# All four heads' probabilities of the second layer's attention are normalised by GpSimd, none by VectorE

## The reference

```python
def _L1_attn_ref(hidden_states, Wq, Wk_down, Wv_down, Wk_up, Wv_up, Wo):
    ...
    scores = jnp.einsum('bhqd,bhkd->bhqk', q, k) * scale
    causal = jnp.tril(jnp.ones((s, s), dtype=bool))
    scores = jnp.where(causal, scores, jnp.asarray(-1000000000.0, scores.dtype))
    attn = jax.nn.softmax(scores, axis=-1)
    out = jnp.einsum('bhqk,bhkd->bhqd', attn, v)
    out = out.transpose(0, 2, 1, 3).reshape(b, s, H * D)
    return out @ Wo.T
```

## Time and profile before

| | |
|---|---|
| median of 3 runs | 2548.25 us |
| profiled execution | 2546.12 us |
| its span, first to last instruction | 2544.3 us |
| mean granted clock of TensorE in the span | 0.956 |
| passes of the second layer's attention | 16, from about 520 to 1438 us and from about 1620 to 2544 us |

### The profile page before, as it was taken

How to read it: one execution, slowest core, us unless ns; L and a number is a source line. 1 busy time by engine, 2 the same in 40 slices (tenths; PEclk the granted TensorE clock), 3 DMA queues, 4 the chain that set the end, 5 groups by cost and what they waited for, 6 DMA issues and landing times. The chain is left out here.

```text
span 2544.3 us, 35763 instructions
## 1 busy us (share of the span) xinstructions
PE 2279.3 (90%) x11666; PEld 1818.9 (71%) x11666; DVE 1551.3 (61%) x3333; ACT 1044.3 (41%) x2182; POOL 917.7 (36%) x957
## 2 busy tenths in 40 slices
PE   5767309799999999999999797899999999999998
PEld 4623107678888888878888685687888888888886
DVE  4289995555656565665656555566565656565665
ACT  3323203344545444444445232344444545454444
POOL 2654214142525243343524101334352525343341
PEclk9879659999999999999999898999999999999999
DMA  9400003801010101010110227201011010101010
GB/s 344 137 0 1 1 35 158 325 31 38 29 49 25 58 8 58 8 58 25 41 50 1 115 92 259 83 9 58 25 41 49 16 49 25 58 8 58 8 46 29
DMA packets 71409, 159.58 MB, mean 63 GB/s; under 512 B 4416, under 2 KB 37568, under 8 KB 64832
## 3 DMA queue, kind: packets, MB, share of 16 engines
q1 hardware_dynamic: 70912, 157.44, 17.8%
q10 hardware_dynamic: 432, 1.32, 0.1%
HBM read 110.52 MB, written 69.99 MB: 71 GB/s over the span
## 5 line engine op out<-in xcount | busy, mean ns | idle before, releaser
L1439 POOL TENSOR_TENSOR probs<-probs,rinv 128x1024 f32<-128x1024 f32 (+7 forms) x384 | 439.1, 1147 | 1117.9 <-DVE rinv L1466 1117.9
L1475 DVE TENSOR_TENSOR pT<-psum,pT 128x512 fp32r<-128x512 f32 x576 | 387.1, 689 | 313.9 <-ACT pT L1515 308.6
L1509 ACT ACTIVATE probs<-psum,nmax 128x256 f32<-128x256 f32 (+7 forms) x512 | 380.7, 743 | 366.9 <-DVE nmax L1461 362.6
L1515 ACT ACTIVATE pT<-psum 128x512 fp32r<-128x512 f32 x576 | 330.3, 595 | 333.3 <-PE psum L1569 332.2
L1461 DVE TENSOR_REDUCE nmax<-psum 128x1 f32<-128x256 f32 (+7 forms) x512 | 378.1, 751 | 48.6 <-PE psum L1558 42.4
L1569 PE MATMUL psum<-ident,probs 128*128 128x128 f32 x2304 | 329.8, 273 | 8.5 <-issue 6.1
L1569 PEld LDWEIGHTS psum<-ident,probs 128*128 128x128 f32 x2304 | 263.2, 141 | 48.5 <-DVE pT L1475 9.0
L93 PE MATMUL psum<-keys,q 128*128 128x512 f32 (+3 forms) x768 | 276.7, 360 | 2.8 <-DVE q L1451 2.8
L93 PE MATMUL psum<-pT,vals 128*128 128x512 f32 x576 | 263.6, 458 | 4.0
L95 PE MATMUL psum<-keys,q 128*128 128x512 f32 (+3 forms) x768 | 262.0, 341 | 0.0
L94 PE MATMUL psum<-keys,q 128*128 128x512 f32 (+3 forms) x768 | 261.7, 341 | 0.0
(11 more groups left out here) (265 smaller groups left out, 3927.1 us busy)
## 6 DMA issues: line engine op xcount, KB each, us to landing
k_parts<-kv_out SPq DMA_DIRECT2D x32, 512.0 KB, 5.1
wq<-wq_copy SPq DMA_DIRECT2D x16, 1024.0 KB, 4.8
wo<-wo_copy SPq DMA_DIRECT2D x16, 1024.0 KB, 4.8
v_parts<-kv_out SPq DMA_DIRECT2D x32, 512.0 KB, 4.0
keys<-k_parts SPq DMA_DIRECT2D x32, 512.0 KB, 4.7
vals<-v_parts SPq DMA_DIRECT2D x64, 256.0 KB, 3.1
acc<-in_x SPq DMA_DIRECT2D x4, 1024.0 KB, 11.9
up_l<-up_copy SPq DMA_DIRECT2D x2, 1024.0 KB, 6.1
```

The costliest lines, as they stand in the source:

```text
L1439: pool.tensor_tensor(p, p, rinv[:, u, h:h + 1].to_broadcast([P, (TB - u) * P]), ALU.mult).then_inc(p_ok, 1)
L1475: dve.tensor_tensor(pT[:, n % PT_SLOTS, 1, :], bank[T_BANK + n % 2], f32(pT[:, n % PT_SLOTS, 0, :]), ALU.subtract).then_inc(t_lo, 1)
L1509: act.activation(probs[:, u % 2, h, 0:n], bank2[2 * (h % 2)][:, off:off + n], ACT.Exp, bias=nmax[:, u, h:h + 1], accum_out=rsum[:, u, h:h ...
L1515: act.activation(pT[:, n % PT_SLOTS, 0, :], bank[T_BANK + n % 2], ACT.Copy).then_inc(t_hi, 1)
```

## The change

GpSimd also multiplies head 3, in the place of the list where norm(u,3) stands. VectorE keeps the four reciprocals and loses the multiplication and its wait. TensorE waits for four counts of `p_ok` for each u in place of three of `p_ok` and one of `p_last`, and the semaphore `p_last` is gone.

```diff
@@ gpsimd
-                    if kind == "norm" and arg[1] < REP - 1:
+                    if kind == "norm":
                         u, h = arg
                         p = probs[:, u % 2, h, 0:(TB - u) * P]
                         pool.wait_ge(p_inv, it * SC + (REP * u + h + 1))
@@ vector
                         dve.reciprocal(rinv[:, u, h:h + 1], rsum[:, u, h:h + 1]).then_inc(p_inv, 1)
-                        if h == REP - 1:
-
-                            p = probs[:, u % 2, h, 0:(TB - u) * P]
-                            dve.wait_ge(p_inv, it * SC + (REP * u + h + 1))
-                            dve.tensor_scalar(p, p, rinv[:, u, h:h + 1], None, ALU.mult).then_inc(p_last, 1)
@@ tensor
                         if k == 0:
-                            pe.wait_ge(p_ok, it * ((REP - 1) * TB) + (REP - 1) * (u + 1))
-                            pe.wait_ge(p_last, it * TB + (u + 1))
+                            pe.wait_ge(p_ok, it * SC + REP * (u + 1))
```

More of the change, by code:

```diff
@@ L1217, in layer1_attention @@
         q_mm, q_hi, q_lo = sem("e_q_mm"), sem("e_q_hi"), sem("e_q_lo")
-        s_mm, s_max, p_exp, p_inv, p_ok, p_last = (sem("e_" + n) for n in ("s_mm", "s_max", "p_exp", "p_inv", "p_ok", "p_last"))
+        s_mm, s_max, p_exp, p_inv, p_ok = (sem("e_" + n) for n in ("s_mm", "s_max", "p_exp", "p_inv", "p_ok"))
         t_mm, t_hi, t_lo, pv_mm = (sem("e_" + n) for n in ("t_mm", "t_hi", "t_lo", "pv_mm"))
```

## The result

| | before | after |
|---|---|---|
| median | 2548.28 us | 2577.43 us |
| runs, lowest to highest | 2543.29 to 2548.75 | 2575.45 to 2580.6 |
| profiled execution, span | 2546.12, 2544.3 us | 2577.52, 2575.7 us |

The ratio is 1.012 with a 95% interval of 1.0103 to 1.0138: the change costs 29 us by the medians. The forecast was 2574, in a range of 2561 to 2582.

A forecast was written before the change was run, and what follows sets the result against it. TensorE was taken as the bound, busy 115.28 of 116 us a pass. Stalls of 12.2 (u = 1), 11.8 (u = 3), 0.3 (u = 0) and 2.7 us (last passes) sum to 27.0 us on 2546.12: 2574, range 2561 to 2582.

The forecast's parts named there:

- Removed: zero in the full passes: VectorE's 128 tensor_scalar instructions go; no wait of TensorE in the full passes stands behind one, so 0 us there.
- u = 1, 0.76 us x 16 = 12.2 us: wo split part 3, queued behind GpSimd's norm(1,3), ends late; project(0)'s weight load stalls 0.76 us in all 16 passes.
- u = 3, 0.84 us x 14 = 11.8 us: GpSimd's norm(3,3) queues behind wq parts 3; the transposition loads 0.84 us late in 14 passes.
- u = 0, 0.02 us x 16: GpSimd's norm queues behind norm(0,2); load possible 882.39 against 882.37, no reserve, 0.3 us in all.
- u = 2, 4, 5, 6 of a full pass, and u = 7: zero: Norms covered: 0.58 us reserve at u = 2, query products at 4 to 6, project(6)'s oT wait at 7.
- The last passes, 1.34 us each: Without query products TensorE waits for GpSimd's longer norms: 0.59, 0.45, 0.30 us at u = 4, 5, 6; 2.7 us together.
- One stall hidden: Rival: one of the two queue stalls, u = 1 or u = 3, is hidden; +15 us, 2561; chance 0.06.
- VectorE's relief: Rival: relief reaches TensorE through the pT subtraction waits, up to 24 us back; about 2540; chance 0.04.
- The whole difference of durations on the path: Rival: GpSimd's longer multiplications all delay the kernel, 128 x 0.56 us = 72 us, 2618; chance 0.01.
- GpSimd stretched in its new places: Rival: other VectorE work stretches GpSimd by 0.45 us at u = 0 and 1; 14 us more, 2588; chance 0.06.
- A balance of half the stalls and a few waits gone: Rival: half the stalls hidden and a few TensorE waits gone leave the time at 2548; chance 0.03.
- GpSimd about twice as slow: Skill's rule for two-input elementwise work against VectorE; trace said to agree, 1.04 against 0.48 us at 512 columns.

## Why the prediction was right, point by point

- **What bounds the kernel.** That a full pass has no more to give held: with VectorE's work left out it took 115.96 us.
- **Removed: zero in the full passes.** Right, shown by the kernel without the multiplication.
- **u = 1, 0.76 us x 16 = 12.2 us.** The mechanism was right to the instruction, the size short: 0.99 us in 14 passes and 0.71 us in two, 15.3 us. The term that was too small is "a released weight load starts about 0.07 us after its releaser". It came from the last pass. In the hardware loop three more waits stand behind `wo_ok` at project(0), and the load starts 0.32 us after the split. The reordered wait gave back 0.27 us.
- **u = 3, 0.84 us x 14 = 11.8 us.** Measured 0.85 us. Both of its inputs held: the split is 1.29 us undisturbed, and GpSimd was on time again at norm(3,1), with 0.78 us of idle ahead of it.
- **u = 0, 0.02 us x 16.** Measured 0.13 us in the full passes, 1.8 us in all. "No reserve" was right, and the norm ended 0.05 us ahead of the load's old place, where the forecast had it. The size failed by the same term as at u = 1: the load starts 0.22 us behind the norm, not 0.07.
- **u = 2, 4, 5, 6 of a full pass, and u = 7: zero.** Right: no stretch that ends at the turns of u = 2, 4, 5 or 6 moved by more than 0.01 us. At u = 7 the weight load does wait 0.19 us for GpSimd and starts 0.14 us later, and the wait of project(6) for oT covers it.
- **The last passes, 1.34 us each.** Measured 0.59, 0.46 and 0.31 us: 1.36.
- **The sum.** 27.0 us forecast, 31.5 us by stretches, 29 us by medians. The 4.5 us missing in the stretches are u = 1 (3.1) and u = 0 (1.5), one term in two places. The forecast of 2574 us came within 3.4 us of the median, nearer than the stretches allow. The difference is luck: the spread of the runs took 2.3 us off the 31.4 us between the traces.
- **The rivals.** One stall hidden: ruled out, they add. VectorE's relief: ruled out. The whole difference of durations on the path: 29 us of 72 (67 us when all eight forms are added up). GpSimd stretched in its new places: its splits are all at 1.04 and 1.3 us. A balance of half the stalls and a few waits gone: neither half appeared.
- **What the profile would show.** VectorE lost 79 us of busy time, not 70: the removed instructions took 0.62 us on average, not 0.55, which no term of the sum used. A full pass grew by 1.96 us, not 1.6, and TensorE's busy time in it by 0.6 us, where none was forecast. The weight load of project(0) is booked as "issue" in the full passes; that the last split releases it shows only with the wait reordered, and in the last passes.
- **GpSimd about twice as slow.** The 1.04 and 0.48 us that the prediction set side by side are two different operations. Against the same two-input form on VectorE, 0.69 us, GpSimd takes 1.5 times as long.

## What to carry to other kernels

Before work is moved to an engine that idles, write down that engine's list in order and look at what stands behind the new entry: here GpSimd idles 60% of a pass, and yet the change cost 15 us because an instruction that waits for a late input was put ahead of a split with a near deadline, and 12 us because another was queued behind a split whose result is needed only later. The order of the list was worth 26 us, the choice of the engine 3 us. When several waits stand ahead of one instruction, look in the trace at which of them the instruction itself carries, and let that be the one that is met last: it isn't always the one that is written last. In the hardware loop the exchange gave back 0.27 us at project(0), and in the last passes the same exchange cost 0.06 us.

## What the runs showed of the hardware

TensorE's queue works its waits off one by one. A weight load followed its releaser by 0.05 us when nothing stood in between, by 0.11 us when the late wait was one instruction ahead of the load, by 0.22 us at u = 0 in the loop, and by 0.32 us with three waits behind the released one at project(0). The profile books such a stall as "issue", though GpSimd caused it; the name appears when the load itself carries the late wait.

A GpSimd instruction that meets a VectorE instruction of the contending kind ends at a fixed distance behind it: 1.04 us became 1.49 and 2.02 us, and both ended 0.9 us behind VectorE's. In three traces the granted clock fell to 0.50 (1.2 GHz) for 3.4 us right behind 1.5 us of idle time of TensorE, and that cost 1.6 us each time.
